# Decoder layer on one core: key weights of batches 3 to 15 formed six or seven batches at once, kept in DRAM

## The reference

```python
# 1. linear attention, 16 heads of 16, K = 2 states multiplied together
q = x + x @ Wq + bq
states = einsum('kbhnd,kbhne->kbhde', ks, vs)   # ks, vs = x + x @ W + b, scaled
out = (layernorm(q @ prod(states)) * ln_g + ln_b) @ Wo + bo
# 2. cross attention, 16 heads of 64, context of 64 keys
q = x @ Wq.T;  k, v = split(ctx @ Wkv.T)
sim = einsum('bhid,bhjd->bhij', q, k) * 64 ** -0.5
out = softmax(where(mask, sim, -big)) @ v @ Wout.T + b_out
# 3. experts: 8 of them, every token goes to each expert up to a capacity of 1024
out = relu(x @ experts_inter[e]) @ experts_out[e] * routing_weight[e]   # summed over e
```

## Time and profile before

| | |
|---|---|
| median of 3 runs | 1288.14 us (1287.87 to 1289.94) |
| the profiled execution | 1288.03 us |
| its span in the profile | 1286.1 us |
| PE busy | 1242.2 us, 97% |
| DVE busy | 876.0 us, 68% |
| ACT busy | 574.5 us, 45% |
| POOL busy | 632.1 us, 49% |
| DMA read and written | 42.29 MB, 26.22 MB |

### The profile page before, as it was taken

The page is one execution under the profiler, slowest core; times in us unless marked ns, Lnnn a source line. Parts: engine busy times, 40 slices in busy tenths (PEclk is TensorE's granted clock), DMA queues, the critical chain, the costliest instruction groups (busy, mean ns, idle before and its releaser), DMA issues.

```text
span 1286.1 us, 22562 instructions
## 1 busy us (share of the span) xinstructions
PE 1242.2 (97%) x8080; PEld 1125.5 (88%) x8080; DVE 876.0 (68%) x1680; ACT 574.5 (45%) x1127; POOL 632.1 (49%) x994
## 2 busy tenths in 40 slices
PE   8968999999999999999999999988989999999997
PEld 7857999999999999999999999877788899899887
DVE  5536988888888889888888888887534323422433
ACT  2124546555565556465555655555514313421421
POOL 2225756757767567567577675664322112102201
PEclk9989999999999999999999999999989999999999
DMA  9831102111121111021111211320210112011001
GB/s 276 203 69 34 42 26 58 33 42 42 34 58 43 34 51 49 28 58 34 42 42 34 57 43 34 97 61 26 91 66 12 56 66 66 1 66 66 1 1 34
DMA packets 117458, 69.98 MB, mean 54 GB/s; under 512 B 74082, under 2 KB 114787, under 8 KB 117348
## 3 DMA queue, kind: packets, MB, share of 16 engines
q1 hardware_dynamic: 115316, 67.87, 18.0%
q10 hardware_dynamic: 2032, 0.66, 0.2%
HBM read 42.29 MB, written 26.22 MB: 53 GB/s over the span
## 4 chain that ended last, share of the span: by engine, by line
PE 86%; DVE 4%; POOL 2%; issue 1%; ACT 1%; POOLq 0%; DVEq 0%
PE ob L137 7%; PE ob L138 7%; PE ob L139 7%; PE sim L137 7%; PE sim L138 7%; PE sim L139 6%; PE pw L417 4%; PE pt L466 4%; PE pw L137 3%; PE pw L139 3%; PE pw L138 3%; PE pw L369 3%; PE pt L137 2%; PE pt L138 2%; PE pt L139 2%; PE pw L393 2%
## 5 line engine op out<-in xcount | busy, mean ns | idle before, releaser
L1518 POOL TENSOR_TENSOR w_lo<-w_raw,w_hi 128x2048 fp32r<-128x2048 f32 x16 | 73.6, 4605 | 230.8 <-ACT w_hi L1454 192.6
L137 PE MATMUL ob<-b_hi,pT_hi 128*128 128x256 f32 x512 | 153.2, 299 | 3.8 <-DVE pT_lo L822 3.8
L139 PE MATMUL ob<-b_hi,pT_lo 128*128 128x256 f32 x512 | 144.8, 283 | 0.0
L138 PE MATMUL ob<-b_lo,pT_hi 128*128 128x256 f32 x512 | 144.8, 283 | 0.0
L902 POOL TENSOR_TENSOR prob<-prob,rz 128x512 f32<-128x512 f32 x128 | 131.0, 1045 | 11.1 <-DVE rz L769 11.1
L684 ACT ACTIVATE prob<-prob 128x512 f32<-128x512 f32 x128 | 80.8, 631 | 112.7 <-DVE prob L815 111.9
L810 DVE TENSOR_REDUCE mx<-sim 128x8 f32<-128x512 f32 x128 | 87.9, 686 | 37.0 <-PE sim L139 35.7
L137 PEld LDWEIGHTS ob<-b_hi,pT_hi 128*128 128x128 f32 x512 | 97.5, 190 | 8.5 <-DVE pT_lo L822 7.8
L596 ACT ACTIVATE x<-h,nmr,rstd 128x256 f32<-128x256 f32 x128 | 76.2, 596 | 63.9 <-POOL nmr L836 59.1
L137 PE MATMUL sim<-a_hi,tT_hi 128*128 128x512 f32 x256 | 104.2, 407 | 0.0
L138 PE MATMUL sim<-a_lo,tT_hi 128*128 128x512 f32 x256 | 101.4, 396 | 0.0
(11 more groups left out here) (243 smaller groups left out, 3880.5 us busy)
## 6 DMA issues: line engine op xcount, KB each, us to landing
xraw<-in_x SPq DMA_DIRECT2D x16, 512.0 KB, 4.0
kv_scratch<-stage SPq DMA_DIRECT2D x32, 256.0 KB, 2.9
x_scratch<-x SPq DMA_DIRECT2D x64, 128.0 KB, 1.7
out_x<-o_sb SPq DMA_DIRECT2D x64, 128.0 KB, 1.7
w_raw<-in_L_ffn_experts_inter SPq DMA_DIRECT2D x8, 1024.0 KB, 5.0
w_raw<-in_L_ffn_experts_out SPq DMA_DIRECT2D x8, 1024.0 KB, 7.6
kraw<-kv_scratch SPq DMA_DIRECT2D x32, 128.0 KB, 3.0
vraw<-kv_scratch SPq DMA_DIRECT2D x32, 128.0 KB, 3.0
```

The lines of the kernel that those rows point to most:

```text
L137: pe.matmul(out, lh, rh, start=first, stop=False)
L138: pe.matmul(out, lh, rl, start=False, stop=False)
L139: return pe.matmul(out, ll, rh, start=False, stop=last)
```

## The change

The A of batch 0 (A0 to A3) is made as before, earlier (iteration -2); those of batches 1 and 2 are made in the same way as C0 to C3 and D0 to D3 in iteration -1, copied by ACT into `a1_stage` and stored to a DRAM array `a_scratch`. For batches 3 to 15 there are 16 units: unit u is head pair u mod 8 of a group of batches, 3 to 8 (384 columns) or 9 to 15 (448 columns). For a unit, SP loads the pair's keys and query weights, each twice into 128 partitions; ACT rounds them (`act_stack`); POOL subtracts (`pool_stack`) so that the upper 64 partitions hold the keys' remainder; two fp32r products per piece, four pieces per unit (U.0 to U.3; the first digit is the slot), then give A without a third pass. ACT copies a piece into `a_stage` (half m = 0 and half m = 1 use the same buffer, so the copy of U.2 and U.3 waits until the DMA store of U.0 and U.1 has landed, and SP stores each half). In slot 3 of each iteration SP reads the next batch's A (two loads of 512 KB) into `a_lo`, ACT rounds it into `a_hi` and DVE subtracts in place. The units stand in slots n = 0, 1, 3, 4, 5, 7, 8, 9, 12, 15, 16, 19, 20, 23, 27 and 31. The mask rows are written into `a_scratch` during setup by 15 DMAs. The order of many other operations in the slots of PE, ACT, DVE and POOL changes too.

```diff
+    UNIT_SLOTS = (0, 1, 3, 4, 5, 7, 8, 9, 12, 15, 16, 19, 20, 23, 27, 31)
+    STACK_SLOTS = (0, 1, 2, 4, 5, 6, 8, 9, 12, 13, 16, 17, 20, 21, 25, 29)
...
+        "G": ((0, 4), (0, 5), (0, 15)), "U01": ((0, 8), (0, 12), (0, 8)),
+        "U00": ((0, 9), (0, 12), (0, 8)), "B0": ((0, 9), (0, 16), (0, 15)),
+        "B1": ((0, 9), (0, 16), (1, 0)), "U02": ((0, 13), (1, 0), (1, 0)),
+        "U03": ((1, 1), (1, 0), (1, 0)), "C1": ((1, 1), (1, 0), (1, 0)),
+        "C0": ((1, 1), (1, 0), (1, 0)), "C2": ((1, 1), (1, 0), (1, 0)),
+        "C3": ((1, 1), (1, 1), (1, 0)), "B3": ((1, 1), (1, 1), (1, 3)),
+        "B2": ((1, 1), (1, 3), (1, 6)), "GT": ((1, 3), (1, 7), (1, 12)),
+        "U10": ((1, 9), (1, 10), (1, 9)), "T1": ((1, 9), (1, 10), (1, 13)),
+        "T0": ((1, 9), (1, 15), (2, 0)), "U11": ((1, 11), (1, 16), (2, 9)),
+        "R": ((1, 13), (2, 0), (2, 14)), "U13": ((1, 13), (2, 1), (2, 9)),
+        "U12": ((1, 13), (2, 1), (2, 9)), "D0": ((2, 0), (2, 4), (2, 9)),
+        "D1": ((2, 1), (2, 5), (2, 9)), "ST": ((2, 8), (2, 11), (2, 17)),
+        "U31": ((2, 9), (2, 19), (3, 3)), "U30": ((3, 1), (3, 1), (3, 3)),
+        "U33": ((3, 1), (3, 3), (3, 3)), "U32": ((3, 2), (3, 4), (3, 3)),
+        "D3": ((3, 2), (3, 4), (3, 9)), "D2": ((3, 2), (3, 4), (3, 9)),
+        "SB": ((3, 6), (3, 9), (3, 8)), "SW": ((3, 6), (3, 12), (3, 15)),
+        "A0": ((0, 8), (0, 10), (0, 9)), "A1": ((2, 4), (1, 13), (1, 9)),
+        "A3": ((2, 12), (2, 17), (2, 9)), "A2": ((3, 1), (3, 12), (3, 9)),
+        "Q1": ((3, 9), (3, 18), (3, 19)), "Q0": ((4, 1), (4, 2), (4, 4))}
...
     def sp_slot(sp, it, slot, e):
+        n = 4 * it + slot
+        if n == -8:
+            sp.dma_start(w_scr.rearrange("r p c -> p r c"), wqx[:, :, 0:C]).then_inc(s["w_stored"], 16)
...
+        if early_pieces(n):
+            store_unit(sp, n, 0)
+        if slot == 3 and it >= 0 and within(it + 1):
+            for h in range(2):
+                sp.wait_ge(s["sim_made"], 2 * n + h + 1)
...
+                sp.dma_start(f32(half(a_lo, h)), a_scr[it + 1, :, :, h * HK:(h + 1) * HK]).then_inc(s[f"a_loaded{h}"], 16)
+        if early_pieces(n):
+            store_unit(sp, n, 1)
...
+        if n == -1:
+            prep_done(sp, -1, last_of("D0", "D1", "D2", "D3"))
+            store_rows(sp, 2)
+            sp.wait_ge(s["rows_stored"], 64)
+            load_unit(sp, 0)
+        for u in stacked_in(n):
+            if u + 1 < 2 * PAIRS:
+                sp.wait_ge(s["stack_made"], u + 1)
+                load_unit(sp, u + 1)
+        if n in UNITS and not early_pieces(n):
+            store_unit(sp, n, 0)
+            store_unit(sp, n, 1)
...
+    def store_unit(sp, n, m):
+        prep_done(sp, n // TPB, last_of(*pieces_of(n)[2 * m:2 * m + 2]))
+        u = UNITS[n]
+        bs, r, p = batches_of(u), u % PAIRS, rows_of(m)
+        sp.dma_start(a_scr[bs, p, m, r * P:(r + 1) * P].rearrange("b p j -> p b j"),
+                     a_stage[p, 0:bs.stop - bs.start, :, :].rearrange("p b e j -> p b (e j)")).then_inc(s[f"a_stored{m}"], 16)
...
+        elif name[0] == "U":
+            u, e, m = unit_of(it, name), int(name[2]) % 2, int(name[2]) // 2
+            g = slice(0, (batches_of(u).stop - batches_of(u).start) * NKV)
+            pe.wait_ge(s["stack_made"], u + 1)
+            c = slice(m * P, (m + 1) * P)
+            pe.matmul(pw[:, g], w_stack_hi[:, e, c], k_stack[:, e, g], start=True, stop=False)
+            last = pe.matmul(pw[:, g], w_stack_lo[:, e, c], k_stack[:, e, g], start=False, stop=True)
...
+            if name[0] == "U":
...
+                need(act, f"a_stored{1 - m}", 16 * (u + m))
...
+    def act_stack(act, u):
+        act.wait_ge(s["r_loaded"], 32 * (u + 1))
...
+        act.activation(k_stack[:, :, g], k_twice[:, :, g], ACT.Copy)
+        act.wait_ge(s["w_loaded"], 32 * (u + 1))
+        act.activation(w_stack_hi[:, :, :], w_twice[:, :, :], ACT.Copy).then_inc(s["stack_hi"], 1)
+    def act_a(act, b, h):
+        act.wait_ge(s[f"a_loaded{h}"], 16 * b)
+        act.activation(half(a_hi, h), f32(half(a_lo, h)), ACT.Copy).then_inc(s["a_hi_made"], 1)
...
+    def dve_a(dve, b, h):
+        dve.wait_ge(s["a_hi_made"], 2 * (b - 1) + h + 1)
+        dve.tensor_tensor(half(a_lo, h), f32(half(a_lo, h)), f32(half(a_hi, h)), ALU.subtract).then_inc(s["a_ready"], 1)
...
+    def pool_stack(pool, u):
+        pool.wait_ge(s["stack_hi"], u + 1)
...
+        pool.tensor_tensor(w_stack_lo[:, :, :], w_twice[:, :, :], f32(w_stack_hi[:, :, :]), ALU.subtract
+                           ).then_inc(s["w_lo_made"], 1)
...
+        pool.tensor_tensor(k_stack[lo, :, g], k_twice[lo, :, g], f32(k_stack[lo, :, g]), ALU.subtract
+                           ).then_inc(s["stack_made"], 1)
...
             if u == PREPS[4]:
                 sp.wait_ge(masked, 2)
                 sp.dma_start(mask_scr, maskrow[:, :]).then_inc(mask_stored, 16)
+                for b in range(1, NB):
+                    sp.dma_start(a_scr[b, 0:1, 0, :].rearrange("p (g j) -> p g j", j=NKV),
+                                 maskrow[:, b * NKV:(b + 1) * NKV].unsqueeze(1).broadcast_to([1, 2 * PAIRS, NKV])
+                                 ).then_inc(mask_stored, 16)
```

More of the change, by code:

```diff
@@ L186, in setup_and_attention, with unit_of, batches_of, pieces_of @@
     sbdT = k.sb("sbdT", [P, MC, P])
+    OLD = 3
+    GROUPS = (slice(OLD, 9), slice(9, NB))
+    GK = max(g.stop - g.start for g in GROUPS) * NKV
+    UNIT_SLOTS = (0, 1, 3, 4, 5, 7, 8, 9, 12, 15, 16, 19, 20, 23, 27, 31)
+    STACK_SLOTS = (0, 1, 2, 4, 5, 6, 8, 9, 12, 13, 16, 17, 20, 21, 25, 29)
+    UNITS = {n: u for u, n in enumerate(UNIT_SLOTS)}
+    assert len(UNITS) == 2 * PAIRS
+    k_stack = k.sb_over("wqx", "k_stack", [P, 2, GK])
+    w_stack_hi = k.sb_at("w_stack_hi", [P, 2, C], F32R, k.offsets["wqx"] + 8 * GK)
+    w_stack_lo = k.sb_at("w_stack_lo", [P, 2, C], F32R, k.offsets["wqx"] + 8 * GK + 8 * C)
+    k_twice = k.sb_over("kraw", "k_twice", [P, 2, GK], F32)
+    a_stage = k.sb_over("w2_raw", "a_stage", [P, GK // NKV, 2, NKV], F32)
+    w_twice = k.sb_at("w_twice", [P, 2, C], F32, k.offsets["w2_raw"] + 8 * GK)
+    a1_stage = k.sb_over("w2_raw", "a1_stage", [P, 2, MC, HK], F32)
+    def unit_of(it, name):
+        return UNITS[TPB * it + int(name[1])]
+    def batches_of(u):
+        return GROUPS[u // PAIRS]
+    def pieces_of(n):
+        return [f"U{n % TPB}{j}" for j in range(4)]
+    def early_pieces(n):
+        return n in UNITS and n % TPB == 3
+    def stacked_in(n):
+        return [u for u, m in enumerate(STACK_SLOTS) if n == m]
     zw_hi = k.sb("zw_hi", [P, 6, P], F32R)
@@ L628, in act_slot @@
         prep(0)
[L629 to L632 removed]
+        for u in stacked_in(n):
+            act_stack(act, u)
         prep(1)
@@ L751, in dve_slot @@
             dve_max(dve, n, 0)
-        prep(2)
         if has_sim:
@@ L884, in pool_slot @@
             pool_rstd_twice(pool, n - 2, q)
+        for u in stacked_in(n):
+            pool_stack(pool, u)
         if slot == SPLIT_SLOT and within(it + 2) and not (isinstance(it, int) and it == -2):
@@ L892, in pool_slot @@
             pool.tensor_tensor(x1_tile, x1_tile, boutbc[:, :], ALU.add).then_inc(s["x1_biased"], 1)
-        if slot == 3 and within(it + 1):
-            need(pool, "v_hi_made", it + 2)
-            pool.tensor_tensor(v_lo[:, :, :], vraw[:, :, :], f32(v_hi[:, :, :]), ALU.subtract).then_inc(s["v_lo_made"], 1)
-        if has_z:
-            pool_rstd(pool, 0, n + 4, q)
         if has_sim:
@@ L903, in pool_slot @@
                                    ALU.mult).then_inc(s["p_ready"], 1)
+        if slot == 3 and within(it + 1):
+            need(pool, "v_hi_made", it + 2)
+            pool.tensor_tensor(v_lo[:, :, :], vraw[:, :, :], f32(v_hi[:, :, :]), ALU.subtract).then_inc(s["v_lo_made"], 1)
+        if tile_exists(n + 5):
+            pool_xb(pool, n + 5, it + 1 if slot < 3 else it + 2, (slot + 1) % 4, par(1 if slot < 3 else 2))
         if has_z:
@@ L912, in pool_slot @@
             ff["pool_small"](pool)
-        if (it, slot) == (NB - 1, 0):
-            ff["pool_weights"](pool, 0, 0, 0)
-    FIRST_PREPS = [n for n in NAMES if enabled(n, -2) and n[0] != "Q"]
+    FIRST_PREPS = [n for n in NAMES if enabled(n, -2) and n[0] not in "AQ"]
     def first_prep(eng, kind, i):
@@ L1151, in _ @@
                     load_wkv(3)
+                if n == 2 * PAIRS + RING:
+                    sp.wait_ge(padded, 2)
+                    for i in range(RING):
+                        sp.wait_ge(staged[i], 16 * (2 * PAIRS // RING))
+                    load_k(sp, 0)
                 if n == 14:
```

263 lines of the change are left out of this document (174 added, 89 removed), and 9 rows, old and new, of the table ORDER.

## The result

The changed kernel takes 1662.3 us (median of 4 runs, 1660.3 to 1662.4) where the kernel before takes 1288.9 us in the same comparison: a ratio of 1.289, 95% interval 1.287 to 1.292. It is 29% slower; a gain of 10 us, to 1278 us, and at most 1293 us had been forecast.

A forecast was written before the change was run, and what follows sets the result against it. The prediction took PE to bound the attention loop: 52.8 us removed, against 24.4 for units, 2 for DVE waits, 11 for store stalls and 4.5 for setup and start, nets -10.9, giving 1278 us; range 1263 to 1293.

The forecast's parts named there:

- L: Time for the store of U.0 and U.1 to land in DRAM after issue: 3.2 us taken, bounds 1.7 and 4.0.
- L - 1.6: PE's stall in us before pT of half 1, in seven slots 3 with a unit: 1.6 each, 11 in all.
- so the landing is covered, nearly: Units of slots 0 and 1: second copies come in the next slot, so the store's landing costs nearly nothing.
- Nothing, if SP isn't late: Reading A back in slot 3: SP's two 512 KB loads land in time for ACT, at no cost.
- The estimate of 3.1 us for 448 KB: Store landing by the skill's rule, about 2.0 us fixed plus bytes at 436 GB/s; would lower the sum by 0.7 us.
- the landing decides: Rival, 0.14: U33's copy waits for the store before exp, 7 us per microsecond of landing; 1294 us at 5.6.
- DVE becomes the bound: Rival, 0.16: DVE's two-SBUF-input subtractions contend with POOL, taking 1.9 to 2.4 us instead of 1.2; 1288 to 1295 us.
- A's pieces: Forming A on PE in each iteration: removing it saves 3.7 us per iteration, 52.8 us in all.
- 16 x 0.205 = 3.3: PE's cost of two units of 448 columns in one iteration, 8 matmuls each; all units cost 24.4 us.
- the ring of four stages gives DVE some 7: Setup: four buffered stages cover most of SP's 8 us for 15 mask DMAs, leaving 0.5 us, bounds 0 and 4.
- 2 + 2 us: Start: 2 us for making A of the first batches early, 2 for the first unit's chain of store and preparation.
- the PE account, 28.4 us of gain in the loop: On PE alone, the loop saves 52.8 us of removed work and pays 24.4 us for the units.

The follow-up runs named there:

- the best version: Changed kernel with half 0 stored as 112 and 15 rows, POOL's `v_lo` earlier, a buffer per half and one mask DMA: 1283.67 us, 0.9964 of the kernel before.
- the three experiments that followed with the same start: On the best version: 14 of 16 units' operands cut to 32 columns, 1284.61 us; DVE's subtraction cut to 32, 1271.72; half 0's subtraction moved to POOL, 1294.09.

## Why the prediction was wrong

**The step that failed** is "L is the unknown of this case", with its bounds of 1.7 and 4.0 us. L was sized by bytes, from stores that all have 128 partitions. For the stores of half 1 this was good: 3.2 forecast, 3.0 and 3.4 measured. The store that the stall hangs on is the other one, of 127 partitions, and landed in 20 to 23 us. The upper bound was no bound: none of its rows has 127 partitions, and the text did not ask whether the shape was like the rows'. From the changed kernel to that with two stores, 1662.3 to 1328.2 us, this is 334 of the 373 us. With L at 20.0 in two units of slots 3 and 22.8 in five, the forecast's own formula, L - 1.6, gives 2 x 18.4 + 5 x 21.2 = 143 us; PE stood 133.5 us there, before SB and not before pT, so this part of the mechanism was right and only its term L was not. The rest is a second step that failed, the cover elsewhere: "so the landing is covered, nearly", said of the units of slots 0 and 1. It did not hold for 20 us (PE waited 111.8 us before the value weights, 69.1 before transposes `tr` and 15.1 in the start), and not quite for 3 (8.9 us). "Nothing, if SP isn't late" failed too: SP was late, by 17 to 20 us. In the changed kernel this was hidden, since ACT stood for the same store (its waits for A are 2.1 us); with buffers of their own it became the larger part. The estimate of 3.1 us for 448 KB, which did not enter the sum, uses a fit that the Trainium skill (DMA: Bandwidth & Descriptors, section Anatomy of one DMA) gives for DMAs issued from GpSimd, while these are issued by SP; at 128 partitions 3.4 and 3.7 us were measured. And in the start one such store holds the first sims: they begin at 135.6 us, 117.8 with two stores, 116.1 before.

**The rival "the landing decides"** (0.14, 1294 us) had the mechanism, and missed both sizes: the landing, and its price, 7 us for each microsecond of L. From two quick stores to 124 and 3 rows L grows by some 5 us and the time by 89, about 18 for each, since all the units wait and not seven. That no gain is left from L = 4.8 us on was not tested by itself: at 3 us there was none either, for the other reasons below.

**The rival "DVE becomes the bound"** (0.16, 1288 to 1295 us) was real as well, beside the other. Its question was 1.2 or 1.9 us a subtraction; the mean was 2.26. Its price was low: it put 0.7 us more per subtraction at 10 us and 1.2 more at 17, and moving one POOL instruction, which took 0.73 us off the mean, gave back 20 us. An iteration without a unit fell from 49.2 to 48.0.

**What the pieces gave.** The matmuls of the units were spaced as forecast, 0.175 to 0.18 us for 384 columns and 0.20 for 448. PE is busy 47.52 us in an iteration without a unit where 46.8 was expected, so A's pieces gave 3.0 us and not 3.7. In the best version an iteration with two units of 448 columns takes 52.75 us, 4.7 more than one without; 16 x 0.205 = 3.3 had been counted for PE. The two stretches of that kernel:

```profile
615.68:663.70 48.02, 47.53 (x308) 42.59 (x307) 43.58 (x84) 27.68 (x57) 35.54 (x59) 1.00 0.20 61
...
312.59:365.34 52.75, 51.17 (x325) 45.71 (x324) 43.58 (x84) 33.95 (x69) 42.32 (x63) 1.00 0.44 118
```

PE's busy time rises by 3.6 us and its idle time from 0.5 to 1.6. Where the 1.1 us of idle time comes from is open. In that version the eight iterations from slot 3 of iteration 0 to slot 3 of iteration 8 take 412.5 us, 28.3 more than eight without a unit and 8.2 more than eight of the kernel before: about 2.2 us for each of some 13 units, where 1.4 to 1.6 had been counted.

**Setup and start.** The masks, 0.5 us forecast with bounds 0 and 4, cost 7: "the ring of four stages gives DVE some 7" us of cover was not there. The start otherwise, 2 + 2 us forecast, was none with quick stores and one mask DMA: the first sims begin at 111.8 us, 4.3 before those of the kernel before (at 113.3 to 115.3 in the three experiments that followed with the same start).

**Hidden as forecast:** POOL's and ACT's work on the stacks.

So the PE account, 28.4 us of gain in the loop, did not come out even with the four flaws mended, though the time, 1283.7 us, lies near the forecast's 1278. From the first sims to the end of the span the best version takes 1169.7 us and the kernel before 1170.0: what A's pieces gave, the units took, and the 4.8 us that are won lie in the start. Of the 379 us between the changed kernel and that one, the 127 rows are 334, POOL's order 20, the shared buffer 18 and the masks 7, taken away in this order; the slow store alone, put back last, is 213, so the shares depend on the order. The step to the buffers of their own goes from one chip to another, on which the kernel before differs by 0.5 us.

## What to carry to other kernels

Before a DMA is sized by its bytes, look at its partition count: a store of 127 rows took six times as long here as one of 128, and splitting it (112 + 15) costs one more issue and wins nearly all of it back. Check that the rows from which a bound is taken have the shape of what is bounded, and treat a slow transfer as one that may also hold the queue behind it. A subtraction with two SBUF inputs on DVE should be put where POOL is idle: taking one POOL operation out of its way won 20 us here, and shrinking it to a sixteenth afterwards 12 more. And a gain in the total should be looked for stretch by stretch: the 4.8 us won here do not come from the loop that the change was made for.

## What the runs showed of the hardware

- A store of 381 KB in pieces of 512 bytes from 127 partitions releases its waiter after 20 us, 444.5 KB after 22.8, with the 16 DMA engines busy for 0.07 of their time; from 124 partitions (372 KB, with 9 KB from 3 more in a second store) after 8.1 us, with 0.24; 392 KB from 112 partitions land in 2.9 us, 448 KB from 128 in 3.4 to 3.7.
- The issue of two loads behind such a store holds SP 17 to 21 us, where it takes 1.2 to 2 us otherwise.
- Fifteen DMAs of one row of 4 KB hold SP 9.4 us; one DMA that writes the same 15 rows, 0.94 us.
- A DVE subtraction of 1024 columns with both inputs in SBUF takes 1.19 us alone and 1.74 to 2.75 beside POOL's operations; POOL's pair of `prob` goes from 2.05 to 3.03 us and `xb` from 0.74 to 1.71 at the same time.
- After PE had stood for 17 us, the clock granted to it was at the lower of its two levels for most of the next 8 us (0.55 of full), where it had been 1.00 before.
